# Linear attention: the gram, gram-query and row products, and the turned input behind them, made of rounded high and low parts

## The chip, the cores and the metric

The kernel runs on one core of one Trainium2 chip. Times are device microseconds of one execution. Beside the plain executions there is one execution recorded by the hardware profiler; rows and spans come from that one.

## The reference

The model is a chain of four layers on X with batch 2, 512 channels and 32x32 positions: deformable attention with an MLP, then a linear attention with a batch norm, then a non-local layer, then a rank-one layer. Only the second is touched:

```
K = conv1x1(X, Wq, bq); Q = conv1x1(X, Wk, bk); V = conv1x1(X, Wv, bv)   # 8 heads of 64 channels, n = 1024
M = einsum('bhmn,bhen->bhme', K, V)
Out = einsum('bhme,bhmn->bhen', M, Q)
Out = conv1x1(Out, Wo, bo) + X
Out = batch_norm over (batch, positions) * gamma + beta
```

There is no softmax between the products, so the kernel never makes K, Q and V. It makes the gram matrix G = X Xᵀ of each batch (512x512, over 1024 positions) and works with that.

## The kernel before

`stage_linear` does this layer. Its work is a list of tasks, `ORDER`, each one accumulation in one PSUM bank; task n uses bank n modulo 8. TensorE runs the list in order. VectorE and ScalarE run over the same list in the same order, and each empties the tasks that are its own. `emptied(engine, n)` makes an engine wait until task n has left its bank; TensorE calls it for task n−8, and for the tasks whose results it reads. Nothing else schedules: the order in the list is the order on every engine, and an engine that waits holds up all that stands behind it. The kinds of tasks, for each batch b:

- `turn` (8): four transposes of 128x128 turn 128 positions of X, so that positions lie on partitions; the copies go to `xt`.
- `gram` (4): row block i of G, columns i·128 to 512 only, so 512, 384, 256 and 128 columns wide, each a sum of 8 plain 32-bit products.
- `mirror` (3): transposes that fill the missing lower blocks of G.
- `row`: the sum of X over positions (`xs`, made by a reduction on VectorE) times Wq, one row.
- `times_q` (4): G times Wq, 4 plain products of 512 columns each; VectorE adds the bias term as it empties them into `gq`.
- `m`: Wv with `gq`, 16 plain products of 128 columns, and a rank-one term with the row `wrow`; VectorE copies the blocks of the heads into `mt`.
- `times_o`, `times_k`: with Wo, then with Wk. `bias_row`, `bias`: the bias that comes along. `y` (8): times X, plus X, with statistics for the batch norm.

Plain products take 32-bit operands. `times_k`, `bias_row` and `y` already work with parts: ScalarE writes a rounded copy of type fp32r (the high part), VectorE writes the operand less that copy, rounded too (the low part), and TensorE adds up high·high, low·high and high·low (`PAIRS`). A task whose result is needed in parts is emptied by both engines, first ScalarE (semaphore `high`), then VectorE.

The trace names memory, not the program's variables. `mlp_w`, `mlp_w_hi`, `Q` and `xn_a` are areas that the stage carves up: before, `xt` and `gram` lie in `mlp_w`, Wq, Wk, Wv and Wo in `mlp_w_hi`, the bias of Wq in `xn_a`. An `_r` behind a name is the same area in the rounded type. `lin_ps` are the eight banks.

Of the kernel before, what the change touches and what calls it, by code (L numbers as in the profile page):

```python
# [1287 lines left out]
def stage_linear(K, sb, ps):  # L1288
# [35 lines left out]
    mm, by_act, by_dve, summed = K.sem("lin_mm"), K.sem("lin_act"), K.sem("lin_dve"), K.sem("x_summed")  # L1324
    high, x_high, x_low, wk_split = K.sem("lin_high"), K.sem("x_high"), K.sem("x_low"), K.sem("wk_split")
# [14 lines left out]
    SPLIT = ("times_o", "times_k")  # L1340
    on_act = [k == "gram" or (k == "turn" and i % 2 == 1) for k, _, i in ORDER]

    def emptied(engine, n):

        engine.wait_ge(by_act if on_act[n] else by_dve, sum(on_act[m] == on_act[n] for m in range(n + 1)))


    TILE_AT = {("times_o", 0, 0): 0, ("times_q", 1, 2): 1, ("y", 0, 4): 2, ("y", 1, 0): 3}
# [5 lines left out]
    with nc.Block() as block:  # L1354
# [15 lines left out]
        def _(pe):  # L1370
            pe.wait_ge(w_in, 96)
            for n, (kind, b, i) in enumerate(ORDER):
# [11 lines left out]
                elif kind == "gram":  # L1384

                    need("turn", PC - 2, PC - 1)
                    for s in range(PC):
                        last = nc.tensor.matmul(out[:, i * P:], xt[b][:, s, i * P:(i + 1) * P], xt[b][:, s, i * P:],
                                                start=(s == 0), stop=(s == PC - 1))
                elif kind == "mirror":  # L1390
                    need("gram", i - 1)
                    for c in range(i):
                        last = nc.tensor.transpose(out[:, c * P:(c + 1) * P], gram[b][:, c, i * P:(i + 1) * P], K.k("ident"))
                elif kind == "row":
                    pe.wait_ge(summed, b + 1)
                    for c in range(CC):
                        last = nc.tensor.matmul(out[0:1, :], xs[:, b, c:c + 1], wq[:, c], start=(c == 0), stop=(c == CC - 1))
                elif kind == "times_q":
                    need("gram", CC - 1)
                    need("mirror", CC - 1)  # L1400
                    for c in range(CC):
                        last = nc.tensor.matmul(out[:], gram[b][:, c, i * P:(i + 1) * P], wq[:, c], start=(c == 0), stop=(c == CC - 1))
                elif kind == "m":
                    need("times_q", CC - 1)
                    need("row", 0)
                    for o in range(CC):
                        part = slice(o * P, (o + 1) * P)
# [25 lines left out]
                elif kind == "y":  # L1433
# [4 lines left out]
                    for c in range(CC):  # L1438
                        for k, (w, x) in enumerate(PAIRS):
                            last = nc.tensor.matmul(out[:], tt[w][:, c, o * P:(o + 1) * P], xp[tile % 2][x][:, c],  # L1440
# [4 lines left out]
        def _(dve):  # L1445
            dve.wait_ge(zero, 1)
            stats = 0
            for n, (kind, b, i) in enumerate(ORDER):
                src = bank[n % 8]
                if kind == "gram" and i == 0:  # L1450
                    nc.vector.tensor_reduce(xs[:, b], K.X[:, :, b], AX.X, ALU.add).then_inc(summed, 1)
                if (kind, b, i) in TILE_AT:
                    tile = TILE_AT[(kind, b, i)]
                    dve.wait_ge(x_high, tile + 1)
                    nc.vector.tensor_tensor(xp[tile % 2][1], x_tile(tile), xp[tile % 2][0].bitcast(F32), ALU.subtract).then_inc(x_low, 1)
# [720 lines left out]
```

## Time and profile before

| | us |
|---|---|
| median of 3 runs | 2783.54 (2780.62 to 2784.2) |
| profiled execution, its time | 2788.09 |
| profiled execution, its span | 2786.3 |
| TensorE busy | 2706.6 (97%) |
| VectorE busy | 2141.4 (77%) |
| ScalarE busy | 1671.4 (60%) |
| mean granted clock of TensorE | 0.99 |

The profiled execution took 2788.09 us, of which 1.8 us lie outside the span. In the rows below, PE is TensorE's products, PEld its loads of the stationary operand, DVE is VectorE, ACT is ScalarE, SP the engine that issues transfers. The first product of the stage starts at 2422.42 us and the first of the next stage at 2604.77 us. A matmul's record is longer than the time until the next one may start, since they run in a pipeline: what one costs in a sequence is the distance between starts.

### The profile page before, as it was taken

The page shows a single profiled execution, that of the slowest core. Times are in us where ns is not written, and L with a number is a line of the kernel's source. Part 1 is how long each engine was busy: PE and PEld are TensorE (multiplying, and loading weights), DVE is VectorE, ACT ScalarE, POOL GpSimd, SP SyncE. Part 2 cuts the span into 40 slices and gives each one's busy share as a digit, 9 for nine tenths or more (in the row PEclk, how much of TensorE's full clock was granted, in tenths as well). Part 3 has the DMA queues.
Part 4 walks back from the last instruction along what each step waited for, and adds up shares of the span by engine and source line. Part 5 has one row for each costly group of instructions (what it writes and reads, how often), then busy time and mean ns, then how long its engine had stood idle before and what let it go on. Part 6 is the DMA issues. An engine that isn't in the chain of part 4 may idle for free. (4 is left out here: it accounts for less than half of the span.)

```text
span 2786.3 us, 45961 instructions
## 1 busy us (share of the span) xinstructions
PE 2706.6 (97%) x20119; PEld 1352.0 (49%) x20119; DVE 2141.4 (77%) x1366; ACT 1671.4 (60%) x2601; POOL 95.4 (3%) x132
## 2 busy tenths in 40 slices
PE   6799999999999999999999999999899999999898
PEld 3434443443443334444444444444578888757653
DVE  4899999999999999999999999999642221224364
ACT  5777777777777777777777777776622222211244
POOL 3000000000000000000000000000431000000000
PEclk9899999999999999999999999999999999999999
DMA  2101000000000000000001010020500000200001
GB/s 72 57 16 30 9 30 30 16 30 9 30 30 16 30 9 30 30 16 30 9 30 30 16 30 9 30 43 1 170 1 1 1 0 1 86 0 1 1 1 61
DMA packets 38760, 72.26 MB, mean 26 GB/s; under 512 B 21088, under 2 KB 22048, under 8 KB 36896
## 3 DMA queue, kind: packets, MB, share of 16 engines
q1 hardware_dynamic: 38496, 69.19, 7.7%
q8 instruction: 158, 2.59, 0.4%
q14 instruction: 42, 0.34, 0.0%
q0 software_dynamic: 64, 0.13, 0.0%
HBM read 60.45 MB, written 8.86 MB: 25 GB/s over the span
## 5 line engine op out<-in xcount | busy, mean ns | idle before, releaser
L862 PE MATMUL l_ps<-mlp_w,W2H 128*64 128x512 f16 x5472 | 913.4, 392 | 1.7 <-DVE mlp_w L888 1.7
L927 ACT ACTIVATE relu_top<-l_ps 128x512 f32<-128x512 f32 x1024 | 611.9, 598 | 416.2 <-PE l_ps L862 371.0
L927 ACT ACTIVATE relu_bottom<-l_ps 128x512 f32<-128x512 f32 x1024 | 612.1, 598 | 79.6 <-PE l_ps L862 1.4
L770 DVE SCALAR_TENSOR_TENSOR relu_top<-relu_bottom,sign_ratio,relu_top 128x2048 f32<-128x2048 f32 x256 | 602.5, 2353 | 11.8 <-PEq L804 6.1
L862 PE MATMUL l_ps<-mlp_w,W2L 128*64 128x512 f16 x2736 | 536.2, 389 | 0.0
L862 PEld LDWEIGHTS l_ps<-mlp_w,W2H 128*64 128x64 f16 x5472 | 304.2, 108 | 357.5 <-issue 78.3
L862 PE MATMUL l_ps<-h_words,W2H 128*64 128x512 f16 x2720 | 453.1, 392 | 0.0
L888 DVE TENSOR_TENSOR mlp_w<-words_x,XN 128x2048 f32<-128x2048 f32 x172 | 392.2, 2292 | 24.6 <-PE l_ps L862 24.6
L888 DVE TENSOR_TENSOR mlp_w<-XN 128x2048 f32<-128x2048 f32 x170 | 387.7, 2294 | 19.3 <-PE l_ps L862 19.0
L862 PE MATMUL l_ps<-h_words,W2L 128*64 128x512 f16 x1360 | 266.1, 388 | 0.0
L764 PE MATMUL l_ps<-relu_top,W 128*32 128x512 f32 x2048 | 246.5, 598 | 0.0
L862 PEld LDWEIGHTS l_ps<-h_words,W2H 128*64 128x64 f16 x2720 | 151.0, 108 | 176.2 <-issue 38.3
L862 PEld LDWEIGHTS l_ps<-mlp_w,W2L 128*64 128x64 f16 x2736 | 153.1, 109 | 120.1 <-issue 0.8
L888 DVE TENSOR_TENSOR h_words<-XN 128x2048 f32<-128x2048 f32 x86 | 197.2, 2294 | 10.6 <-PE l_ps L862 10.6
L888 DVE TENSOR_TENSOR h_words<-words_x,XN 128x2048 f32<-128x2048 f32 x84 | 192.5, 2292 | 12.8 <-PE l_ps L862 12.8
L1280 DVE TENSOR_TENSOR KV_diag_r<-mlp_ps,KV_diag_r 128x512 fp32r<-128x512 f32 x43 | 29.7, 692 | 188.5 <-ACT mlp_ps L1262 188.5
L1261 ACT ACTIVATE KV_diag_r<-mlp_ps,vecs 128x512 fp32r<-128x512 f32 x43 | 29.6, 688 | 175.5 <-PE mlp_ps L1230 175.5
L764 PEld LDWEIGHTS l_ps<-relu_top,W 128*32 128x32 f32 x2048 | 53.2, 109 | 131.9 <-issue 129.0
L851 PE MATMUL l_ps<-XN,y_weights_halves 12*128 12x512 bf16 x1024 | 101.3, 385 | 7.8 <-PEq L382 7.8
L862 PEld LDWEIGHTS l_ps<-h_words,W2L 128*64 128x64 f16 x1360 | 76.0, 108 | 59.5
L851 PE MATMUL l_ps<-y_rows,y_weights_halves 12*128 12x512 bf16 x1024 | 101.1, 384 | 0.0
L851 PEld LDWEIGHTS l_ps<-XN,y_weights_halves 12*128 12x128 bf16 x1024 | 25.9, 91 | 143.6 <-issue 139.8
(392 smaller groups left out, 2695.9 us busy)
## 6 DMA issues: line engine op xcount, KB each, us to landing
XN<-pos_table SPq DMA_DIRECT2D x64, 512.0 KB, 3.8
mlp_w<-in_mlp_w SPq DMA_DIRECT2D x8, 1024.0 KB, 9.5
X<-in_x SPq DMA_DIRECT2D x8, 512.0 KB, 7.6
bias_scratch<-XN SPq DMA_DIRECT2D x64, 64.0 KB, 2.0
XN<-bias_scratch SPq DMA_DIRECT2D x16, 256.0 KB, 5.6
out<-Q SPq DMA_DIRECT2D x16, 256.0 KB, 2.2
XN<-y_pieces SPq DMA_DIRECT2D x96, 12.0 KB
y_rows<-y_pieces SPq DMA_DIRECT2D x96, 12.0 KB
```

Source lines behind the costliest of these rows:

```text
L764: last = nc.tensor.matmul(p3[32 * q:32 * q + 32, :], K.W3[:, 30 - 2 * n:62 - 2 * n], tops[i % 3][:, r, BANK * u:BANK * (u + 1)], start=(n ...
L770: nc.vector.scalar_tensor_tensor(tops[i % 3], bots[i % 2][:], K.RHO[:], tops[i % 3], ALU.mult, ALU.add).then_inc(folded, 1)
L851: last = nc.tensor.matmul(out[q][:], K.WYD[32 * q:32 * q + YROWS, q % 2], yr[bg % 2][32 * q:32 * q + YROWS, y] .unsqueeze(1).to_broadcast( ...
L862: last = nc.tensor.matmul(out[q][a * DH:(a + 1) * DH, :], w[:, half], h[a][:, :, k], start=False, stop=stop, tile_position=(0, a * DH))
L888: nc.vector.tensor_tensor(hw[i % 3][:, r].rearrange("p (m j) -> p m j", j=J), words_x, words_y[:, 2 * n + r].unsqueeze(1).to_broadcast([P, ...
L927: nc.scalar.activation((bots[i % 2] if d else tops[i % 3])[:, r, BANK * u:BANK * (u + 1)], banks[BANK_OF[c % PER]][:], ACT.Relu).then_inc( ...
L1261: nc.scalar.activation(hid[n % SLOTS][0], pa[n % 3][:], ACT.Gelu, bias=K.v("mlp_b1", f))
L1280: nc.vector.tensor_tensor(lo, pa[n % 3][:], hi.bitcast(F32), ALU.subtract).then_inc(lo_done, 1)
```

## The change

- `turn` and `gram` join the kinds that are emptied in two parts, by ScalarE and then VectorE. Before, ScalarE emptied all `gram` tasks and every second `turn` task alone, VectorE the other `turn` tasks. The high parts of the turned X lie in `Q`, the low ones in `mlp_w`.
- `gram` and `times_q` are three products of parts for each plain one. Wq is split for it, once: the high part by ScalarE before gram (1,0), the low part by VectorE before the first mirror of batch 0.
- `mirror` turns both parts: 6 tasks a batch instead of 3.
- `row` is one task for both batches. `xs` now holds the sums of batch 0 in column 0 and of batch 1 in column 32 of 33, the rest zeros, so that the two results land on partitions 0 and 32. It too is three products of parts. It stands directly in front of `m` of batch 0.
- The two reductions over X move from before gram (0,0) and (1,0) to before gram (0,2) and (1,1) in VectorE's order.
- The last six `turn` tasks of batch 1 move between the grams of batch 0.
- The split of tile 1 of X for `y` moves from `times_q` (1,2) to `times_k` (0,0), since its memory holds a part of the gram until then.
- All waits on emptied tasks now count VectorE's semaphore alone.

```
+    low, rest = carver(K.w_lo), carver(K.w_hi2)
+    xt = [[low([P, PC, C]) for _ in range(B)], [rest([P, PC, C]) for _ in range(B)]]
+    gram = [[low([P, CC, C]) for _ in range(B)], [aT[1], xp[0][0]]]
+    wqp = [carver(K.w_hi2)([P, CC, C]), K.w_hi[:, 0:2].rearrange("p f a o -> p (f a) o")]
...
-    ORDER = (tasks("turn", 0, *range(PC)) + tasks("turn", 1, *range(PC)) + tasks("gram", 0, *range(CC)) + tasks("row", 0, 0)
-             + tasks("gram", 1, 0) + tasks("mirror", 0, *range(1, CC)) + tasks("gram", 1, 1) + tasks("times_q", 0, *range(CC))
-             + tasks("gram", 1, 2, 3) + tasks("m", 0, 0) + tasks("row", 1, 0) + tasks("mirror", 1, *range(1, CC))
+    MIRROR = [(k, part) for k in range(1, CC) for part in range(2)]
+    ORDER = (tasks("turn", 0, *range(PC)) + tasks("turn", 1, *range(2)) + tasks("gram", 0, 0) + tasks("turn", 1, *range(2, 5))
+             + tasks("gram", 0, 1) + tasks("turn", 1, *range(5, PC)) + tasks("gram", 0, 2, 3)
+             + tasks("gram", 1, 0) + tasks("mirror", 0, *range(len(MIRROR))) + tasks("gram", 1, 1) + tasks("times_q", 0, *range(CC))
+             + tasks("gram", 1, 2, 3) + tasks("row", 0, 0) + tasks("m", 0, 0) + tasks("mirror", 1, *range(len(MIRROR)))
...
-    SPLIT = ("times_o", "times_k")
+    SPLIT = ("turn", "gram", "times_o", "times_k")
...
-                    need("turn", PC - 2, PC - 1)
+                    need("turn", PC - 1)
                     for s in range(PC):
-                        last = nc.tensor.matmul(out[:, i * P:], xt[b][:, s, i * P:(i + 1) * P], xt[b][:, s, i * P:],
-                                                start=(s == 0), stop=(s == PC - 1))
+                        for k, (w, x) in enumerate(PAIRS):
+                            last = nc.tensor.matmul(out[:, i * P:], xt[w][b][:, s, i * P:(i + 1) * P], xt[x][b][:, s, i * P:],
+                                                    start=(s == 0 and k == 0), stop=(s == PC - 1 and k == 2))
...
-                    pe.wait_ge(summed, b + 1)
+                    pe.wait_ge(summed, B + 3)
+                    pe.wait_ge(wq_split, 2)
                     for c in range(CC):
-                        last = nc.tensor.matmul(out[0:1, :], xs[:, b, c:c + 1], wq[:, c], start=(c == 0), stop=(c == CC - 1))
+                        for k, (w, x) in enumerate(PAIRS):
+                            last = nc.tensor.matmul(out[0:33, :], xsp[w][:, c], wqp[x][:, c], start=(c == 0 and k == 0), stop=(c == CC - 1 and k == 2))
...
-                        last = nc.tensor.matmul(out[:], gram[b][:, c, i * P:(i + 1) * P], wq[:, c], start=(c == 0), stop=(c == CC - 1))
+                        for k, (w, x) in enumerate(PAIRS):
+                            last = nc.tensor.matmul(out[:], gram[w][b][:, c, i * P:(i + 1) * P], wqp[x][:, c],
+                                                    start=(c == 0 and k == 0), stop=(c == CC - 1 and k == 2))
...
-                    need("row", 0)
+                    emptied(pe, AT[("row", 0, 0)])
...
+                if (kind, b, i) in (("gram", 0, 2), ("gram", 1, 1)):
+                    nc.vector.tensor_reduce(xs[:, :, b, 0], K.X[:, :, b], AX.X, ALU.add).then_inc(summed, 1)
...
+                if (kind, b, i) == ("mirror", 0, 0):
+                    dve.wait_ge(wq_split, 1)
+                    nc.vector.tensor_tensor(wqp[1], wq, wqp[0].bitcast(F32), ALU.subtract).then_inc(wq_split, 1)
```

The beginning of the stage on TensorE, before (L1383 is `turn`, L1388 `gram`, L1397 `row`, L1393 `mirror`):

```order
L1383 MATMUL lin_ps<-consts_sb,X 128x128 x64
L1388 MATMUL lin_ps<-mlp_w 128x512 x8
L1388 MATMUL lin_ps<-mlp_w 128x384 x8
L1388 MATMUL lin_ps<-mlp_w 128x256 x8
L1388 MATMUL lin_ps<-mlp_w 128x128 x8
L1397 MATMUL lin_ps<-mlp_w_hi,x_sums 1x512 x4
L1388 MATMUL lin_ps<-mlp_w 128x512 x8
```

The same place after (L1399 is `turn`, L1405 `gram`; a gram task of 8 steps is eight times the three rows):

```order
L1399 MATMUL lin_ps<-consts_sb,X 128x128 x40
L1405 MATMUL lin_ps<-mlp_w_r 128x512
L1405 MATMUL lin_ps<-mlp_w_r,Q_r 128x512
L1405 MATMUL lin_ps<-Q_r,mlp_w_r 128x512
...
L1399 MATMUL lin_ps<-consts_sb,X 128x128 x12
L1405 MATMUL lin_ps<-mlp_w_r 128x384
```

Gram (0,0) now follows ten turn tiles instead of sixteen, and every plain product is three.

VectorE in the front part of the stage, before (L1464 empties `turn`, L1451 sums X, L1458 and L1459 make low parts of the bias and of Wk, L1468 empties `row`, L1466 `mirror`, L1471 `times_q`):

```order
L1464 COPY mlp_w<-lin_ps 128x512 x8
L1451 TENSOR_REDUCE x_sums<-X 128x4
L1458 TENSOR_TENSOR bk_part<-vecs,bk_part 128x4
L1459 TENSOR_TENSOR mlp_w_hi_r<-mlp_w_hi,xn_a_r 128x2048
L1468 SCALAR_TENSOR_TENSOR wq_s<-xn_a,lin_ps 1x512
L1451 TENSOR_REDUCE x_sums<-X 128x4
L1466 COPY mlp_w<-lin_ps 128x128
L1466 COPY mlp_w<-lin_ps 128x256
L1466 COPY mlp_w<-lin_ps 128x384
L1471 SCALAR_TENSOR_TENSOR mlp_w<-xn_a,x_sums,lin_ps 128x512 x4
```

And after, from gram (0,2) on (L1477 sums X, L1509 writes low parts, L1483 the low part of Wq, L1495 empties `mirror`, L1500 `times_q`):

```order
L1477 TENSOR_REDUCE x_sums<-X 128x4
L1509 TENSOR_TENSOR mlp_w_r<-lin_ps,mlp_w_r 128x256
L1509 TENSOR_TENSOR mlp_w_r<-lin_ps,mlp_w_r 128x128
L1509 TENSOR_TENSOR mlp_w_r<-lin_ps,mlp_w_r 128x512
L1483 TENSOR_TENSOR mlp_w_hi_r<-mlp_w_hi,Q_r 128x2048
L1495 CAST mlp_w_r<-lin_ps 128x128 x2
L1495 CAST mlp_w_r<-lin_ps 128x256 x2
L1495 CAST mlp_w_r<-lin_ps 128x384 x2
L1477 TENSOR_REDUCE x_sums<-X 128x4
L1509 TENSOR_TENSOR mlp_w_r<-lin_ps,mlp_w_r 128x384
L1500 SCALAR_TENSOR_TENSOR mlp_w<-xn_a,x_sums,lin_ps 128x512 x4
```

The low part of Wq and six mirror copies now stand between gram (1,0) and the second sum over X.

TensorE around `m` of batch 0, before (L1409 and L1410 are `m`, L1402 `times_q`; four pairs of the two `m` rows):

```order
L1388 MATMUL lin_ps<-mlp_w 128x128 x8
L1409 MATMUL lin_ps<-mlp_w,mlp_w_hi 128x128 x4
L1410 MATMUL lin_ps<-wq_s,xn_a 128x128
...
L1397 MATMUL lin_ps<-mlp_w_hi,x_sums 1x512 x4
L1393 MATMUL lin_ps<-consts_sb,mlp_w 128x128 x6
L1402 MATMUL lin_ps<-mlp_w_hi,mlp_w 128x512 x8
```

And after (L1417 is `row`, L1433 and L1434 `m`, L1411 `mirror`, L1424 `times_q`):

```order
L1417 MATMUL lin_ps<-Q_r,x_sums_part 33x512 x2
L1417 MATMUL lin_ps<-mlp_w_hi_r,x_sums_part 33x512
...
L1433 MATMUL lin_ps<-mlp_w,mlp_w_hi 128x128 x4
L1434 MATMUL lin_ps<-wq_s,xn_a 128x128
...
L1411 MATMUL lin_ps<-consts_sb,mlp_w_r 128x128 x12
L1424 MATMUL lin_ps<-Q_r,mlp_w_r 128x512 x2
```

The row task stood behind `m` of batch 0 for batch 1; now it stands in front of it, and `m` is followed at once by the transposes.

## Rows read from the trace of the kernel before

**Rows 1.** The page: busy time, then busy tenths and granted clock in 40 slices.

```profile
PE 2706.6 (97%) x20119; PEld 1352.0 (49%) x20119; DVE 2141.4 (77%) x1366; ACT 1671.4 (60%) x2601; POOL 95.4 (3%) x132
...
PE   6799999999999999999999999999899999999898
...
PEclk9899999999999999999999999999999999999999
```

**Rows 2.** Timeline, TensorE: start us, length us, engine, line, operation, shapes, count, idle before.

```profile
2422.42 10.15 PE L1383 MATMUL lin_ps<-consts_sb,X 128*128 128x128 f32 x64 [3.09 <-PEq L1200]
...
2432.41 17.43 PE L1388 MATMUL lin_ps<-mlp_w 128*128 128x512 f32 x64
2449.77 3.59 PE L1397 MATMUL lin_ps<-mlp_w_hi,x_sums 128*1 128x512 f32 x8
2453.29 7.13 PE L1388 MATMUL lin_ps<-mlp_w 128*128 128x512 f32 x16
2460.26 0.82 PE L1393 MATMUL lin_ps<-consts_sb,mlp_w 128*128 128x128 f32 x6
2460.92 5.32 PE L1388 MATMUL lin_ps<-mlp_w 128*128 128x384 f32 x16
2466.08 13.90 PE L1402 MATMUL lin_ps<-mlp_w_hi,mlp_w 128*128 128x512 f32 x32
2479.82 5.40 PE L1388 MATMUL lin_ps<-mlp_w 128*128 128x256 f32 x32
...
2490.96 3.59 PE L1397 MATMUL lin_ps<-mlp_w_hi,x_sums 128*1 128x512 f32 x8
...
2496.41 7.11 PE L1402 MATMUL lin_ps<-mlp_w_hi,mlp_w 128*128 128x512 f32 x16 [1.05 <-DVE mlp_w L1466]
```

**Rows 3.** Timeline, TensorE, products of rounded parts: `times_k` (L1419) and `y` (L1440).

```profile
2513.89 0.39 PE L1419 MATMUL lin_ps<-aT_hi,mlp_w_hi_r 128*128 128x512 f32 x1
...
2524.61 0.39 PE L1419 MATMUL lin_ps<-mlp_w_r,xn_a_r 128*128 128x512 f32 x1
...
2575.35 22.04 PE L1440 MATMUL lin_ps<-mlp_w_r 128*128 128x512 f32 x96 [0.55 <-DVE lin_bias L1484]
```

**Rows 4.** Weight loads: timeline; then groups (count, busy us, mean ns, idle before).

```profile
2479.82 5.21 PEld L1388 LDWEIGHTS lin_ps<-mlp_w 128*128 128x128 f32 x31 [0.24 <-issue]
...
L1419 PEld LDWEIGHTS lin_ps<-aT_hi,xn_a_r 128*128 128x128 f32 x32 | 6.0, 188 | 1.6 <-issue 0.2
```

**Rows 5.** Timeline, VectorE: sum of X, low part of Wk, evictions.

```profile
2432.78 4.41 DVE L1451 TENSOR_REDUCE x_sums<-X 128x4 f32<-128x4096 f32 x1
...
2437.18 2.28 DVE L1459 TENSOR_TENSOR mlp_w_hi_r<-mlp_w_hi,xn_a_r 128x2048 fp32r<-128x2048 f32 x1
...
2453.40 0.68 DVE L1468 SCALAR_TENSOR_TENSOR wq_s<-xn_a,lin_ps 1x512 f32<-1x512 f32 x1 [13.94 <-PE lin_ps L1397]
...
2491.07 0.42 DVE L1475 COPY mt<-lin_ps 64x256 f32<-64x256 f32 x1 [10.30 <-PE lin_ps L1410]
...
2495.20 1.07 DVE L1466 COPY mlp_w<-lin_ps 128x128 f32<-128x128 f32 x3
...
2506.42 2.48 DVE L1480 TENSOR_TENSOR mlp_w_r<-lin_ps,aT_hi 128x512 fp32r<-128x512 f32 x4
```

**Rows 6.** Timeline, ScalarE: turn tiles 4, 6, 8 and 10 leave their banks.

```profile
2426.11 0.60 ACT L1528 ACTIVATE mlp_w<-lin_ps 128x512 f32<-128x512 f32 x1 [1.11 <-PE lin_ps L1383]
2427.81 0.60 ACT L1528 ACTIVATE mlp_w<-lin_ps 128x512 f32<-128x512 f32 x1 [1.11 <-PE lin_ps L1383]
2429.10 0.60 ACT L1528 ACTIVATE mlp_w<-lin_ps 128x512 f32<-128x512 f32 x1 [0.69 <-PE lin_ps L1383]
2429.98 0.60 ACT L1528 ACTIVATE mlp_w<-lin_ps 128x512 f32<-128x512 f32 x1 [0.28 <-PE lin_ps L1383]
```

**Rows 7.** Busy us (count) of stretches; then granted clock, DMA share, GB/s.

```profile
2422.37:2432.35 9.98, 9.93 (x64) 9.96 (x65) 5.02 (x8) 4.18 (x7) 0.52 (x1) 0.69 0.42 127
2432.35:2449.77 17.42, 17.42 (x68) 10.94 (x65) 7.11 (x4) 3.97 (x6) 0.00 (x0) 1.00 0.00 0
```

More of the change, by code:

```diff
@@ L1303, in stage_linear @@
     room = carver(K.WR)
-    xt, gram = [room([P, PC, C]) for _ in range(B)], [room([P, CC, C]) for _ in range(B)]
+    room([P, B * (PC + CC), C])
     gq = room([P, CC, C])
-    room([P, CC, C])
     mt = sb("mt", [P, CC, P])
@@ L1339, in stage_linear, with parts @@
     PAIRS = ((0, 0), (1, 0), (0, 1))
-    SPLIT = ("times_o", "times_k")
-    on_act = [k == "gram" or (k == "turn" and i % 2 == 1) for k, _, i in ORDER]
+    SPLIT = ("turn", "gram", "times_o", "times_k")
     def emptied(engine, n):
-        engine.wait_ge(by_act if on_act[n] else by_dve, sum(on_act[m] == on_act[n] for m in range(n + 1)))
-    TILE_AT = {("times_o", 0, 0): 0, ("times_q", 1, 2): 1, ("y", 0, 4): 2, ("y", 1, 0): 3}
+        engine.wait_ge(by_dve, n + 1)
+    def parts(kind, b, i):
+        if kind == "turn":
+            return [xt[p][b][:, i] for p in range(2)]
+        if kind == "gram":
+            return [gram[p][b][:, i, i * P:] for p in range(2)]
+        return [{"times_o": aT, "times_k": tt}[kind][p][:, i] for p in range(2)]
+    TILE_AT = {("times_o", 0, 0): 0, ("times_k", 0, 0): 1, ("y", 0, 4): 2, ("y", 1, 0): 3}
+    FREE = {0: ("gram", 1, CC - 1), 1: ("times_q", 1, CC - 1), 2: ("y", 0, CC - 1), 3: ("y", 0, 2 * CC - 1)}
+    xsum = flat(xs[:]).rearrange("p (c k) -> p c k", c=CC)[:, :, 0:33]
     def x_tile(tile):
@@ L1390, in _ @@
                 elif kind == "mirror":
-                    need("gram", i - 1)
-                    for c in range(i):
-                        last = nc.tensor.transpose(out[:, c * P:(c + 1) * P], gram[b][:, c, i * P:(i + 1) * P], K.k("ident"))
+                    k, part = MIRROR[i]
+                    need("gram", k - 1)
+                    for c in range(k):
+                        last = nc.tensor.transpose(out[:, c * P:(c + 1) * P], gram[part][b][:, c, k * P:(k + 1) * P].bitcast(F32), K.k("ident"))
@@ L1409, in _ @@
                             nc.tensor.matmul(out[:, part], wv[:, c, part], gq[:, c, part], start=(c == 0), stop=False)
-                        last = nc.tensor.matmul(out[:, part], bvr[0:1, part], wrow[:, part], start=False, stop=True)
+                        last = nc.tensor.matmul(out[:, part], bvr[at, part], wrow[at, part], start=False, stop=True)
                 elif kind == "times_o":
@@ L1439, in _ @@
                         for k, (w, x) in enumerate(PAIRS):
[L1440 removed]
+                            last = nc.tensor.matmul(out[:], tt[w][:, c, o * P:(o + 1) * P], xp[(tile + 1) % 2][x][:, c],
                                                     start=(c == 0 and k == 0), stop=(c == CC - 1 and k == 2))
@@ L1446, in _ @@
             dve.wait_ge(zero, 1)
+            nc.vector.memset(xs[:], 0.0).then_inc(summed, 1)
+            dve.wait_ge(summed, 1)
             stats = 0
@@ L1477, in _ @@
                 elif kind in SPLIT:
-                    part = {"times_o": aT, "times_k": tt}[kind]
+                    part = parts(kind, b, i)
                     dve.wait_ge(high, sum(k in SPLIT for k, _, _ in ORDER[:n + 1]))
-                    nc.vector.tensor_tensor(part[1][:, i], src[:], part[0][:, i].bitcast(F32), ALU.subtract).then_inc(by_dve, 1)
+                    nc.vector.tensor_tensor(part[1], src[:, i * P if kind == "gram" else 0:], part[0].bitcast(F32), ALU.subtract).then_inc(by_dve, 1)
                 elif kind == "bias_row":
@@ L1522, in _ @@
                 src = bank[n % 8][:]
-                if on_act[n]:
+                if kind in SPLIT:
                     act.wait_ge(mm, n + 1)
-                    if kind == "gram":
-                        nc.scalar.activation(gram[b][:, i, i * P:], src[:, i * P:], ACT.Copy).then_inc(by_act, 1)
-                    else:
-                        nc.scalar.activation(xt[b][:, i], src, ACT.Copy).then_inc(by_act, 1)
-                elif kind in SPLIT:
-                    act.wait_ge(mm, n + 1)
-                    nc.scalar.activation({"times_o": aT, "times_k": tt}[kind][0][:, i], src, ACT.Copy).then_inc(high, 1)
+                    nc.scalar.activation(parts(kind, b, i)[0], src[:, i * P if kind == "gram" else 0:], ACT.Copy).then_inc(high, 1)
             N_ST = CC * B * NT + CC
```

44 lines of the change are left out of this document (26 added, 18 removed).

## The prediction, made before the changed kernel ran

> **What bounds the kernel now.** The page came first. TensorE is busy for 97% of the span, and its granted clock is nine tenths or more in 39 of 40 slices [rows 1]. So time leaves the kernel where TensorE's own work gets shorter, and comes in where it waits. The diff touches one stage, the linear attention, which runs from 2422.4 us to about 2604.8 us. Next I read the timeline of TensorE in that stage [rows 2]. The reader is to see that its records follow each other without a hole from 2422.42 to 2496.41, where the only wait in the part that changes stands: 1.05 us, for VectorE's mirror copies. VectorE and ScalarE are mostly idle there: in 17.42 us of the first gram products VectorE works 7.11 us and ScalarE 3.97 us [rows 7]. So extra evictions have room, unless someone waits for them.
>
> **The price of a product.** A plain 32-bit product leaves two records in the trace. The 16 records of 384 columns from 2460.92 to 2466.08 are 0.3225 us apart, and 16 of 256 plus 16 of 128 columns take 5.23 us from 2479.82 to 2485.05: plain records scale with the columns, 0.429, 0.322, 0.215 and 0.107 us for 512, 384, 256 and 128 (0.429 from the 32 in the 13.74 us from 2466.08); the six transposes at 2460.26, (0.82−0.27)/5, are 0.11 us apiece [rows 2]. A product of rounded parts leaves one record. In the products that are split already (48 of `times_k`, 46 steps from 2513.89 to 2524.61) it takes 10.72/46 = 0.233 us; in `y` (95 steps in 22.04 minus one length of 0.39) 0.228 us [rows 3]. Three of them for 512 columns cost 0.70 us against 0.858 us plain: 18% less, not a third.
>
> All those rows have 512 columns. At 2.4 GHz, 512 columns are 0.213 us, so 0.020 us is left over for each. I take the same surplus for narrower ones: 0.180 us for 384 and 0.127 us for 256 columns. For 128 columns that would be 0.073 us, but each product has a weight load of its own, and 31 loads of 128 columns went by in 5.21 us at steps down to 0.107 us beside the plain records [rows 4]; no row shows them closer. I take 0.107 us. The bounds: from below, 0.053 us (pure streaming at 128 columns); from above, what a whole plain product of that width costs, 0.215 us for 128 and 0.429 us for 256 columns.
>
> The Trainium skill ("TensorE: Matmul & The Clock Gate", "LDWEIGHTS (loading the stationary operand)") puts a load at its columns over 1.2 GHz, 107 ns for 128; the trace's loads last 188 ns each but follow at 0.107 us, which agrees with it as a rate. The same page ("Back-to-back issue gap") gives columns over 2.4 GHz plus 2.5 ns, 216 ns for 512; the rows have 228 to 233 ns. The measurement decides.
>
> **Part by part, on TensorE.**
> - `times_q`: 32 products of 512 columns. 64 records of 0.429 us are 27.5 us; 96 of 0.233 us are 22.4 us. −5.1 us.
> - `row`: two tasks of 3.52 us each (2449.77 to 2453.29, and again at 2490.96) [rows 2] become one of 12 records, 2.8 us. −4.2 us.
> - `gram`: 16 products of each width. 512: 13.7 to 11.2 us. 384: 10.3 to 8.6. 256: 6.9 to 6.1. 128: 3.4 to 5.1, dearer, since three loads take the place of two records. Together −3.3 us.
> - `mirror`: both parts are transposed, 12 transposes more at 0.11 us. +1.3 us.
> - `turn`: the same 64 transposes. `m`, `times_o`, `times_k`, `y`: untouched.
>
> **The waits that it adds.** Every turn and gram tile now passes through ScalarE (high part, 0.60 us) and then VectorE (low part, 0.69 us; back to back (2.48−0.69)/3 = 0.60 us each [rows 5]), where before one of them copied it. In the opening (granted clock 0.69 over the first 10 us [rows 7]) two turn tiles take TensorE 1.70 us, 2426.11 to 2427.81 [rows 6], 0.85 us each, so the two keep up.
> - Gram of batch 0 now starts after ten turn tiles and needs tile 8. ScalarE began on that tile at 2429.10 and on the tenth at 2429.98 [rows 6]. So the high part ends at 2429.70, the low part at 2430.5, TensorE resumes at 2430.6, and has been idle since 2429.8: +0.8 us. The six turn tiles put between the grams cost what they cost before.
> - `m` of batch 0 stands directly behind `row`, and waits for VectorE's 0.68 us on it [rows 5]. The record's end lags TensorE's next start by 0.16 us; with about 0.15 us of hand-over that is +1.0 us. Before, gram products and others lay between. Queued behind that wait is all of TensorE.
> - Before `times_q` of batch 1 six mirror copies stand where three stood: three take 1.07 us. From the end of `m`: 0.1, the two copies of `mt` 0.85, six copies 2.1, hand-over 0.1, 3.2 us; TensorE's transposes end at 1.5. A wait of 1.7 us instead of 1.05: +0.7 us.
> - Batch 0's `times_q` has cover, just: from the end of gram (1,0), its low part is done at +1.3 us, the low part of Wq (2.28 us as for Wk [rows 5]) at +3.6, six copies at +5.7; TensorE has mirrors 1.3 and gram (1,1) 4.3, so 5.6 us. About 0. What comes late here goes onto the path one for one.
> - The two sums over X (4.41 us each [rows 5]) now stand before the low parts of gram (0,2) and gram (1,1). The first hides behind the rest of that gram and the 5.6 us of gram (1,0), the second behind four `times_q` of 2.8 us and free banks. 0, and up to 4.4 us each without that cover.
> - The memset, the parts of the sums (128x132) and Wq's high part lie beside TensorE's work: 0.
> - The split of x tile 2 moves from `times_q` to `times_k` of batch 0; its first user is `y` of the second tile, over 20 us later: 0. No DMA moves.
>
> Sum: −5.1 −4.2 −3.3 +1.3 +0.8 +1.0 +0.7 = **−8.8 us**. The stage behind 2513.25 slides forward unchanged. Against the profiled execution, 2788.1 us with its frame, that gives 2779.3 us; the median of the runs shown is 4.5 us lower, so 2774.7 us.
>
> **The rivals.**
> 1. *Narrow rounded products cost a whole plain product at 128 columns.* Nothing in the trace shows a rounded product below 512 columns. At 0.215 us instead of 0.107 for 48 records: +5.2 us, gain 3.6 us, 2779.9 us. For: they are weight-bound there already and nothing shows the rate. Against: the loads of plain records do better.
> 2. *The penalty reaches 256 columns too.* 48 records at 0.429 instead of 0.127 us: another +14.5 us; in all +10.9 us, 2794.4 us, slower. It decides once the 96 records of 256 and 128 columns cost 0.092 us more each than I take.
> 3. *VectorE becomes the bound in the front part.* It gets about 16 turn low parts, 8 gram low parts, 6 more mirror copies and Wq, some 20 us more in 70 us. If the tight place before `times_q` slips by 3 us, the gain is 5.8 us: 2777.7 us.
> 4. *Loads do not bind.* 128 columns at 0.053 us (−2.6 us) and 0.228 us or its surplus elsewhere (252 records by 0.005, −1.3 us): gain 12.7 us, 2770.8 us. The skill's issue-gap rule, cited above, points this way: by it the sum would be some 4 us better than mine even with loads at 107 ns. Rows 3 speak against it.
> 5. *The change does not do what it says.* The order of instructions shows 192 gram products and 96 of `times_q`, each with rounded operands on both sides, so only the rate can fail.
>
> **How the numbers follow.** Forecast (−8.8 us) 45%, rival 1 32%, rival 2 7%, rival 3 10%, rival 4 6%. The three runs before spread over 3.6 us, so I widen the ends by 1 to 2 us: 2771 to 2782.5 us holds the forecast, rivals 1 and 3 and half of 4. About 0.2% (5.6 us) is what a measurement of this kernel tells from no change. Faster by more: nearly all of the forecast, half of 3, all of 4: 52%. Within: nearly all of 1, half of 3, a little of the forecast: 38%. Slower: rival 2 and a rest: 10%.
>
> **What would show it.** In the changed trace: `times_k` starts at about 2504.5 instead of 2513.25 us. Gram records 0.233, 0.18, 0.127 and 0.107 us apart by width; 0.21 at 128 is rival 1, 0.4 at 256 rival 2. Waits of TensorE of about 0.8 us before the first gram record, 1.0 before `m`, 1.7 before `times_q` of batch 1, and none over 0.3 before that of batch 0. A low granted clock behind 2430 us would make all of it wrong, as would a lasting queue of full banks.

## The result, and the profile after

| | before | after |
|---|---|---|
| median of 14 runs each | 2783.36 us (2780.62 to 2785.43) | 2775.42 us (2773.24 to 2778.83) |
| profiled execution | 2788.09 us | 2777.56 us |
| its span | 2786.3 us | 2775.7 us |
| first transpose of the stage to second `times_k` record | 2422.42 to 2513.89 = 91.47 us | 2422.08 to 2503.21 = 81.13 us |

The changed kernel takes 0.9972 of the time before, 95% interval 0.9964 to 0.9979: 7.9 us less, 5.8 to 10.0. The forecast was 8.8 us less, 2774.7 us.

The page of after, first part (busy us, share, instructions):

```profile
PE 2693.2 (97%) x20223; PEld 1364.2 (49%) x20223; DVE 2153.3 (78%) x1390; ACT 1678.5 (60%) x2611; POOL 95.4 (3%) x132
```

Against [rows 1], TensorE has 104 records more and 13.4 us less busy time. VectorE has 24 instructions and 11.9 us more. A count of instructions alone says nothing here: a wide rounded record costs less than one of the two that a plain product leaves (0.227 for 0.429 us at 512 columns, below).

TensorE's timeline in the stage, after (columns as in [rows 2]):

```profile
2422.08 5.91 PE L1399 MATMUL lin_ps<-consts_sb,X 128*128 128x128 f32 x40 [3.08 <-PEq L1200]
2429.44 0.47 PE L1405 MATMUL lin_ps<-mlp_w_r 128*128 128x512 f32 x1 [1.45 <-DVE Q_r L1509]
...
2432.51 0.39 PE L1405 MATMUL lin_ps<-mlp_w_r,Q_r 128*128 128x512 f32 x1
...
2434.78 0.39 PE L1405 MATMUL lin_ps<-Q_r,mlp_w_r 128*128 128x512 f32 x1
2435.01 1.48 PE L1399 MATMUL lin_ps<-consts_sb,X 128*128 128x128 f32 x12
...
2437.91 0.33 PE L1405 MATMUL lin_ps<-mlp_w_r 128*128 128x384 f32 x1
...
2440.17 0.33 PE L1405 MATMUL lin_ps<-mlp_w_r,Q_r 128*128 128x384 f32 x1
...
2442.07 0.28 PE L1405 MATMUL lin_ps<-Q_r,mlp_w_r 128*128 128x256 f32 x1
...
2444.58 0.28 PE L1405 MATMUL lin_ps<-Q_r,mlp_w_r 128*128 128x256 f32 x1
...
2444.88 0.27 PE L1405 MATMUL lin_ps<-Q_r,mlp_w_r 128*128 128x128 f32 x1
...
2447.22 0.28 PE L1405 MATMUL lin_ps<-Q_r,mlp_w_r 128*128 128x128 f32 x1
...
2458.91 0.70 PE L1424 MATMUL lin_ps<-Q_r,mlp_w_r 128*128 128x512 f32 x2 [0.37 <-DVE mlp_w_r L1495]
...
2475.42 0.62 PE L1417 MATMUL lin_ps<-Q_r,x_sums_part 128*33 128x512 f32 x2
...
2477.95 0.40 PE L1417 MATMUL lin_ps<-mlp_w_hi_r,x_sums_part 128*33 128x512 f32 x1
2479.21 1.13 PE L1433 MATMUL lin_ps<-mlp_w,mlp_w_hi 128*128 128x128 f32 x8 [0.86 <-DVE wq_s L1497]
...
2485.19 1.54 PE L1411 MATMUL lin_ps<-consts_sb,mlp_w_r 128*128 128x128 f32 x12
...
2488.52 0.70 PE L1424 MATMUL lin_ps<-Q_r,mlp_w_r 128*128 128x512 f32 x2 [1.80 <-DVE mlp_w_r L1495]
...
2494.07 3.60 PE L1437 MATMUL lin_ps<-mlp_w_hi,mt 128*128 128x512 f32 x8
...
2503.21 0.39 PE L1443 MATMUL lin_ps<-aT_hi,mlp_w_hi_r 128*128 128x512 f32 x1
```

Start minus start, divided by the steps between two records of one width, is the price of a product of rounded parts:

| columns | rows | steps | us each | forecast | two plain records, a third of it |
|---|---|---|---|---|---|
| 512 | 2432.51 to 2434.78 | 10 | 0.227 | 0.233 | 0.286 |
| 384 | 2437.91 to 2440.17 | 13 | 0.174 | 0.180 | 0.215 |
| 256 | 2442.07 to 2444.58 | 21 | 0.120 | 0.127 | 0.143 |
| 128 | 2444.88 to 2447.22 | 21 | 0.111 | 0.107 | 0.074 |

The last column is the price at which the split would break even. The three wide forms are under it, the narrowest one is above it: there the split loses. The steps are those of the even part of each task. Over the whole of a task, from its first record to the first one behind it, the 24 products of each width took 5.57, 4.27, 2.95 and 2.63 us, so 0.232, 0.178, 0.123 and 0.110 us each: the first wide products of a task stand further apart.

The group of waits says where TensorE stands idle in the stage (us in total, times, longest); before, it had only one wait in the part that changes [rows 2]:

```profile
PE lin_ps L1399 <- PEq L1200: 3.1, 1, 3.1
PE lin_ps L1424 <- DVE mlp_w_r L1495: 2.2, 2, 1.8
PE lin_ps L1405 <- DVE Q_r L1509: 1.4, 1, 1.4
PE lin_ps L1433 <- DVE wq_s L1497: 0.9, 1, 0.9
```

The first is there before the change too and stands ahead of the stage's first transpose. The other three lines are four waits, together 4.5 us, against 1.05 us before. All four are for VectorE.

### The profile page after: what moved, and what is told of

It reads as the page before. It is cut to its first block and busy times, and to the rows that moved or that the text cites. A ratio compares the mean times of both kernels' runs of the same rounds, so it can differ in the third digit from the quotient of the medians.

```text
span 2775.7 us, 46239 instructions
## 1 busy us (share of the span) xinstructions
PE 2693.2 (97%) x20223; PEld 1364.2 (49%) x20223; DVE 2153.3 (78%) x1390; ACT 1678.5 (60%) x2611; POOL 95.4 (3%) x132
## 5 line engine op out<-in xcount | busy, mean ns | idle before, releaser
L770 DVE SCALAR_TENSOR_TENSOR relu_top<-relu_bottom,sign_ratio,relu_top 128x2048 f32<-128x2048 f32 x256 | 601.2, 2348 | 11.9 <-PEq L804 6.1
```

What stands on the lines that cost most here:

```text
L770: nc.vector.scalar_tensor_tensor(tops[i % 3], bots[i % 2][:], K.RHO[:], tops[i % 3], ALU.mult, ALU.add).then_inc(folded, 1)
```

## The experiments

Each ran beside the kernel before on the same chip. The edits named "on after" start from the changed kernel, "on before" from the kernel before. Two measures are used. The ratio of medians has an interval of 2 to 4 us on either side. The stage front, from the first transpose to the second record of `times_k` in one profile, is finer and holds all that the change touches. It holds the moment at which the granted clock rises as well: in eleven of the twelve profiles 2.8 to 3.7 us after the stage's first transpose, in the first profile of before 6.1 us after it.

### Both kernels again

No edit.

> The kernel before, unchanged, profiled once more. The changed kernel's turn tiles reached the full granted clock about 3.5 us earlier than in the first profile of before (40 transposes in 5.9 us, where before needed about 7.4 us for them). Theory: that moment varies from run to run, and the change has nothing to do with it; then this profile may show another moment than 2428.4 us. Rival: the change brings it forward; then this profile again shows the half clock until about 2428 us, and 64 transposes in 9.9 to 10.2 us.

> The changed kernel, unchanged. Time 7.0 to 8.5 us under before. If the moment of the clock's rise varies by itself, the 40 first transposes may take anything from 5.9 to 7.4 us here, and the wait before the first gram product then goes the other way, 1.45 us with an early rise and 0.8 us with a late one; the stage up to times_k then takes 80.9 to 81.7 us. If the change brings it forward, they take 5.9 us again.

Measured: 2782.28 us (one run), and 2775.96 us, ratio 0.997 [0.996, 0.9981]. Stage front 89.96 and 81.10 us. Before, again, TensorE's timeline:

```profile
2419.88 8.65 PE L1383 MATMUL lin_ps<-consts_sb,X 128*128 128x128 f32 x64 [3.08 <-PEq L1200]
...
2509.84 0.39 PE L1419 MATMUL lin_ps<-aT_hi,mlp_w_hi_r 128*128 128x512 f32 x1
```

The same 64 transposes took 10.15 us in the first profile [rows 2]. The granted clock explains it. Windows of before again, then of the first profile of before (window; its length; busy us and count of PE, PEld, DVE, ACT, POOL; granted clock; DMA share; GB/s):

```profile
2421.80:2422.80 1.00, 1.00 (x7) 1.00 (x6) 0.09 (x1) 0.60 (x1) 0.00 (x0) 0.50 0.85 320
2422.80:2423.80 1.00, 1.00 (x11) 1.00 (x10) 0.65 (x2) 0.49 (x1) 0.00 (x0) 0.96 0.90 256
```

```profile
2426.00:2428.00 2.00, 2.00 (x12) 2.00 (x11) 0.69 (x1) 0.78 (x2) 0.00 (x0) 0.50 0.87 284
2428.00:2430.00 2.00, 2.00 (x17) 2.00 (x17) 1.15 (x2) 1.03 (x3) 0.00 (x0) 0.88 0.06 19
```

In the first profile the clock was at 0.50 (1.2 GHz) until about 2428.5 (0.48 us of the stretch from 2428 give its mean of 0.88), 6.1 us after the first transpose. In before again it rose 3.0 us after it, in after 2.8 us. So 1.5 us of the 10.3 us between the first two profiles (91.47 − 81.13) is a late rise in one execution. With the early rise in both, the change takes 89.96 − 81.10 = **8.9 us** out of the stage front.

### Plain products put back, gram alone and `times_q` alone

On after:

```diff
-for k, (w, x) in enumerate(PAIRS):
-    last = nc.tensor.matmul(out[:, i * P:], xt[w][b][:, s, i * P:(i + 1) * P], xt[x][b][:, s, i * P:], ...)
+last = nc.tensor.matmul(out[:, i * P:], xt[0][b][:, s, i * P:(i + 1) * P].bitcast(F32), xt[0][b][:, s, i * P:].bitcast(F32), ...)
```

> The changed kernel, but each gram product is one plain 32-bit product on the high part of X alone; the low parts of X are made and not used, so the gram lacks them. Theory: TensorE's rate is what counts. Plain records cost 0.858, 0.644, 0.429 and 0.215 us a product, three rounded ones in the changed kernel's trace 0.683, 0.520, 0.360 and 0.334 us; 16 products of each: +2.8, +2.0, +1.1 and -1.9 us, together +4.0 us over the changed kernel; 0.4 us of it are taken back, since the wait before times_q of batch 0 vanishes. So 4.2 us under before. Rival, that the gain of the gram was eaten by waits and evictions: no slower than the changed kernel, 7.9 us under before.

And for the other:

```diff
-for k, (w, x) in enumerate(PAIRS):
-    last = nc.tensor.matmul(out[:], gram[w][b][:, c, i * P:(i + 1) * P], wqp[x][:, c], ...)
+last = nc.tensor.matmul(out[:], gram[0][b][:, c, i * P:(i + 1) * P].bitcast(F32), wqp[0][:, c].bitcast(F32), ...)
```

> The changed kernel, but times_q is one plain product for each, on the high parts of the gram and of Wq; the low parts are made and not used there. Theory: 32 products at 0.858 instead of 0.683 us, +5.6 us over the changed kernel, 2.3 us under before. Rival, that times_q waits for VectorE's evictions or the sums over X and not for its own products: under +2 us.

Measured: gram plain 2779.19 us (0.9983 [0.9974, 0.9993]), 3.2 us above after again; stage front 86.28 us, 5.2 us more. `times_q` plain 2780.99 us (0.9988 [0.9979, 0.9998]), 5.0 us above; stage front 86.78 us, 5.7 us more. The 16 products of batch 0 are one row of TensorE's timeline, 32 records in 13.97 us, as in the kernel before (13.90 [rows 2]), and the wait ahead is the one of after:

```profile
2456.63 13.97 PE L1423 MATMUL lin_ps<-Q_r,mlp_w_r 128*128 128x512 f32 x32 [0.37 <-DVE mlp_w_r L1493]
```

The profile of gram plain did not fit its own median (2782.16 for 2779.19 us). The surplus is not in the gram. It stands in the windows behind the wait before `times_q` of batch 1 (columns as in the windows above):

```profile
2492.00:2494.00 2.00, 1.44 (x6) 1.25 (x7) 0.30 (x1) 0.00 (x0) 0.00 (x0) 0.97 0.00 0
2494.00:2496.00 2.00, 2.00 (x6) 1.52 (x6) 0.00 (x0) 0.00 (x0) 0.00 (x0) 0.50 0.00 0
2496.00:2498.00 2.00, 2.00 (x8) 1.57 (x7) 0.75 (x1) 0.00 (x0) 0.00 (x0) 0.67 0.00 0
2498.00:2500.00 2.00, 2.00 (x10) 1.60 (x9) 0.05 (x1) 0.00 (x0) 0.00 (x0) 1.00 0.00 0
```

TensorE's timeline at that place, of the same kernel:

```profile
2492.56 0.71 PE L1423 MATMUL lin_ps<-Q_r,mlp_w_r 128*128 128x512 f32 x2 [1.80 <-DVE mlp_w_r L1494]
...
2494.98 0.63 PE L1423 MATMUL lin_ps<-mlp_w_hi_r,mlp_w_r 128*128 128x512 f32 x1
```

The granted clock fell to 0.50 for about 3.4 us, and the records got longer (0.63 for 0.39 us). That cost 1.65 us: the two `times_q` tasks took 7.19 us (2492.56 to 2499.75) instead of the 5.55 us of after. Is it caused by plain gram products, or does it come and go? The same kernel was run again for that:

> The variant with plain gram products on the high parts, profiled once more. In its first profile the granted clock fell to half for 3.4 us behind TensorE's wait of 1.8 us, which cost 1.65 us; four profiles with the same wait had no such fall. Theory: chance decides, and this profile most likely shows none, with 84.6 us from the first transpose to the second record of times_k instead of 86.3 us. Rival: this kernel always has it, then 86.3 us again.

Measured: 2781.05 us (one run), stage front 84.67 us, 3.57 us above after again, and no fall of the clock.

```profile
2421.58 6.23 PE L1399 MATMUL lin_ps<-consts_sb,X 128*128 128x128 f32 x40 [3.08 <-PEq L1200]
...
2506.25 0.39 PE L1442 MATMUL lin_ps<-aT_hi,mlp_w_hi_r 128*128 128x512 f32 x1
```

So the split of `times_q` is worth 5.7 us and that of the gram 3.6 us. The 3.6 us are net: with plain gram products the wait ahead of `times_q` of batch 0 is gone, and with split ones it costs 0.5 us. The same edit ran without the fall of the clock, so the edit does not force it.

### The row product once, on before

```diff
-+ tasks("gram", 0, *range(CC)) + tasks("row", 0, 0)
++ tasks("gram", 0, *range(CC))
...
-+ tasks("gram", 1, 2, 3) + tasks("m", 0, 0) + tasks("row", 1, 0) + tasks("mirror", 1, ...)
++ tasks("gram", 1, 2, 3) + tasks("row", 0, 0) + tasks("m", 0, 0) + tasks("mirror", 1, ...)
...
-last = nc.tensor.matmul(out[0:1, :], xs[:, b, c:c + 1], wq[:, c], ...)
+last = nc.tensor.matmul(out[0:33, :], xsum[:, c], wq[:, c], ...)
```

> The kernel before with one part of the change alone: the row product made once for both batches (33 columns, plain products), in front of m of batch 0. Theory, with the steps of the prediction: the second row task goes (-3.5 us), m now waits for VectorE's eviction of the row (+1.0 us), and the wait before times_q of batch 1 grows by 0.2 us, since no row covers the mirror copies: -2.3 us, 2781.2 us if before is 2783.5. Rival, merging is free of new waits: -3.5 us. Rival, it pays nothing, because the second row had hidden the mirror copies: 0.

Measured: 2783.59 us, 0.9997 [0.9988, 1.0007], which is −0.3 us with an interval of −3.3 to +1.9. By the median this part alone can't be told from nothing. Its stage front is 87.89 us against 89.96 of before again, −2.1 us. The granted clock rose 3.7 us after the first transpose here, for 3.0 us, and the 64 transposes took 0.2 us longer (8.70 for 8.49 us, start to start): −2.3 us at an equal opening, as forecast. TensorE's timeline:

```profile
2478.18 3.62 PE L1399 MATMUL lin_ps<-mlp_w_hi,x_sums 128*33 128x512 f32 x8
...
2482.67 1.13 PE L1412 MATMUL lin_ps<-mlp_w,mlp_w_hi 128*128 128x128 f32 x8 [0.86 <-DVE wq_s L1473]
...
2490.88 7.11 PE L1404 MATMUL lin_ps<-mlp_w_hi,mlp_w 128*128 128x512 f32 x16 [1.35 <-DVE mlp_w L1471]
```

One row product of 33 stationary columns takes 3.62 us, as long as one of a single column (3.59 [rows 2]). The second one goes. Behind the one that is left there is the wait for VectorE, 0.86 us, and the wait before `times_q` of batch 1 is longer (1.35 for 1.05 us). −3.5 us for the product that goes, and about 1.2 us back in two waits.

### The waits taken away by order

Row product ahead of the last gram task, and the mirrors ahead of `m`, on after:

```diff
-+ tasks("gram", 1, 2, 3) + tasks("row", 0, 0) + tasks("m", 0, 0) + tasks("mirror", 1, *range(len(MIRROR)))
++ tasks("gram", 1, 2) + tasks("row", 0, 0) + tasks("gram", 1, 3) + tasks("mirror", 1, *range(len(MIRROR))) + tasks("m", 0, 0)
```

> The changed kernel with another order: gram (1,2), row, gram (1,3), the six mirrors of batch 1, and only then m of batch 0. Theory: the waits of 0.86 us (m for the row) and 1.80 us (times_q of batch 1 for the mirror copies) are pure loss and both go: 2.7 us under the changed kernel, 2773.3 us, 10.2 us under before. In the trace no wait of TensorE over 0.2 us between gram (1,2) and times_o. Rival: the waits come back elsewhere (at gram (1,3)'s bank, or at times_q of batch 1 for the low part of gram (1,3)): gain under 1 us.

Five turn tiles of batch 1 ahead of the first gram, and Wq's low part made later on VectorE, on after:

```diff
-+ tasks("turn", 1, *range(2)) + tasks("gram", 0, 0) + tasks("turn", 1, *range(2, 5)) + tasks("gram", 0, 1)
++ tasks("turn", 1, *range(5)) + tasks("gram", 0, 0) + tasks("gram", 0, 1)
...
-if (kind, b, i) == ("mirror", 0, 0):
+if (kind, b, i) == ("gram", 1, 0):
     dve.wait_ge(wq_split, 1)
```

> The changed kernel with five turn tiles of batch 1 instead of two before gram (0,0), and VectorE's low part of Wq before its low part of gram (1,0). Theory: TensorE does three more turn tiles (1.3 us) while it waits for VectorE's low part of tile 8, so of the wait of 1.4 us 0.1 to 0.2 us are left; and the 0.37 us before times_q of batch 0 go: 1.6 us under the changed kernel, 2774.4 us. Rival: VectorE is the bound of the opening, and gram (0,1) then waits for what it has to do: gain under 0.5 us.

Both together:

> The changed kernel with both reorderings. If they are independent, 4.3 us under the changed kernel: 2771.7 us, 11.8 us or 0.42% under before. If the two sets of waits share a cause, no better than the better of the two. In a profile of another variant the granted clock fell to half for 3.4 us right behind the wait of 1.8 us, at a cost of 1.6 us; without that wait no such fall can stand there, so the mean gain may be larger than the sum of the waits.

| | median | ratio to before | stage front | against after again (81.10) | expected |
|---|---|---|---|---|---|
| row and mirrors moved | 2772.84 | 0.9959 [0.9946, 0.9973] | 78.12 | −3.0 | −2.7 |
| turn tiles and Wq moved | 2774.50 | 0.9968 [0.9956, 0.9980] | 79.28 | −1.8 | −1.6 |
| all moved | 2769.98 | 0.9949 [0.9937, 0.9962] | 76.12 | −5.0 | −4.3 |

What the two give adds up (3.0 + 1.8 = 4.8 of 5.0 us): the waits are separate and none was hidden behind another. With all moved, the group of TensorE's waits in the stage has one line left, the one ahead of it:

```profile
PE lin_ps L1399 <- PEq L1200: 3.1, 1, 3.1
```

TensorE's timeline of all moved shows the four places without a bracket, so without idle time over 0.15 us ahead: the first gram record, `times_q` of batch 0, `m` behind the mirrors, and `times_q` of batch 1:

```profile
2420.16 7.30 PE L1399 MATMUL lin_ps<-consts_sb,X 128*128 128x128 f32 x52 [3.08 <-PEq L1200]
2427.52 0.47 PE L1405 MATMUL lin_ps<-mlp_w_r 128*128 128x512 f32 x1
...
2455.14 0.63 PE L1424 MATMUL lin_ps<-Q_r,mlp_w_r 128*128 128x512 f32 x2
...
2474.31 1.50 PE L1411 MATMUL lin_ps<-consts_sb,mlp_w_r 128*128 128x128 f32 x12
...
2475.65 1.06 PE L1433 MATMUL lin_ps<-mlp_w,mlp_w_hi 128*128 128x128 f32 x8
...
2481.55 0.73 PE L1424 MATMUL lin_ps<-Q_r,mlp_w_r 128*128 128x512 f32 x2
```

This is the version that beats both kernels: 2769.98 us (2768.98 to 2770.98), some 14 us below the 2783.93 of before beside it, and 5.4 us below the 2775.42 of after (which had before at 2783.36 beside it). VectorE does the same work in it, only not while TensorE stands waiting.

### What the narrowest product waits for

Is the 0.111 us of a 128-column product its weight load? On after, the narrowest gram task loads half as many columns; all 128 columns still stream. The lower half of that gram block is left out, so the time is that of less data loaded, not of the reference's work. The edit halves the output rows along with the load; the two are not told apart.

```diff
+m = P // 2 if i == CC - 1 else P
...
-last = nc.tensor.matmul(out[:, i * P:], xt[w][b][:, s, i * P:(i + 1) * P], xt[x][b][:, s, i * P:], ...)
+last = nc.tensor.matmul(out[0:m, i * P:], xt[w][b][:, s, i * P:i * P + m], xt[x][b][:, s, i * P:], ...)
```

> The changed kernel, but the products of the narrowest gram tasks (128 columns) load only 64 of the 128 stationary columns; the lower half of that block of the gram is left out. In the changed kernel's trace these records are 0.111 us apart, 256 columns 0.120, 384 columns 0.173 and 512 columns 0.2275: all but the narrowest are columns over 2.4 GHz plus 0.0135 us, which would give 0.067 us for 128. Theory: the narrowest wait for their weight loads; with half the load they come down to about 0.067 us. Rival, a floor per product that has nothing to do with the load: 0.111 us as before.

Measured: 2771.68 us (one run), stage front 78.71 us, 2.4 us less than after again. TensorE's timeline, the narrowest gram task:

```profile
2441.86 0.22 PE L1406 MATMUL lin_ps<-mlp_w_r 128*64 128x128 f32 x1
...
2443.24 0.23 PE L1406 MATMUL lin_ps<-Q_r,mlp_w_r 128*64 128x128 f32 x1
```

23 steps in 1.38 us, 0.060 us each, where the same moving columns took 0.111 us. So the stationary width, and not the moving one, sets the pace at 128 columns. What sets it at 0.060 us is open: half the load and 128 streamed columns come to the same 0.053 us. And 0.060 is less than the 0.067 us that the expectation made of the surplus of 0.0135 us, so that surplus does not hold for every form. The loads of that line (shortest, median and longest ns of one record):

```profile
L1406 PEld LDWEIGHTS lin_ps<-mlp_w_r x64: 134/188/192, 2426.6 to 2469.9; 128*128 128x128 f32 x48, 128*64 128x64 f32 x16
```

A load's record of 188 ns is much longer than the 111 ns between loads, so its length is no price: the next one begins before it ends. The Trainium skill ("TensorE: Matmul & The Clock Gate", "LDWEIGHTS (loading the stationary operand)") puts a load at its columns over 1.2 GHz, so 107 and 53 ns. Steps of 111 and 60 ns are 4 and 13% above that.

## Why the prediction was right, point by point

| term | forecast | measured | from |
|---|---|---|---|
| `times_q` | −5.1 | −5.3 to −5.7 | two tasks in 5.55 us (2488.52 to 2494.07), four such pairs, against 27.5; and `times_q` plain |
| row once and split | −4.2 | −4.3 | 2.76 us for 7.04; 12 records from 2475.42 |
| gram | −3.3 | −3.9, −3.6 | its four tasks 15.42 for 17.36 us in a batch; gram plain, net of the wait behind it |
| mirrors | +1.3 | +1.3 | batch 1: 12 transposes in 1.54 us (row at 2485.19) for 6 in 0.87; batch 0: 1.48 for 0.82 |
| wait before gram (0,0) | +0.8 | +1.4 to +1.6 | row at 2429.44; 1.6 by starts |
| wait before `times_q`, batch 0 | 0 | +0.5 | last gram record at 2458.21 plus a step of 0.17, to 2458.91 |
| `m` behind row | +1.0 | +1.0 | 2477.95 plus one step, 2478.18, to the start of `m` at 2479.21 |
| wait before `times_q`, batch 1 | +0.7 | +0.75 | 1.80 for 1.05 us |
| sum | −8.8 | −8.4 to −9.0 | stage front at equal clock: −8.9 |

An idle time in brackets counts from the end of a record, about 0.16 us behind the moment at which the next one could have started, so a wait that is new costs that much more than its bracket: 0.53 us for 0.37, 1.03 for 0.86.

That the sum agrees to 0.1 us is luck in part. The products came out cheaper than forecast by 0.6 us in the gram and 0.2 to 0.6 us in `times_q`, and two waits dearer by 0.6 to 0.8 and 0.5 us; the errors took each other out.

**The price of wide rounded products.** The method was right: take the surplus over pure streaming from a row that exists, and carry it to widths that no row shows. The surplus was mis-sized. It is 0.0135 us rather than 0.020 in the even part of a task: 0.227, 0.174 and 0.120 us are 512, 384 and 256 columns at 2.4 GHz (0.213, 0.160, 0.107) plus 0.0135. The row that I took it from (0.233 [rows 3]) and `y` in the same group (0.228) already disagreed. I took the dearer one, and the cheaper one was the general case. Here it was worth 0.6 us of the gram term.

**The narrow product.** Bound by the stationary side, 0.111 us for a forecast of 0.107. The forecast read the plain records too low: those of 128 columns do not stand 0.107 us apart, and 0.215 us is not the price of a product. In the kernel before, the last gram task of batch 1 has 15 steps from 2483.27 to 2484.94, 0.1115 us each and 0.223 us a product, and its loads follow each other at 0.110 to 0.112 us. So the trace of before held the measured rate. The 0.107 came out of the assumption that plain records scale with their columns down to 128. Rival 1 (0.215) is excluded by the rows, and rival 2 (0.429 at 256 columns) as well. The half load shows that the cause is on the stationary side. Rival 4 fell with its main term: narrow products do not run at 0.053 us. Its smaller one, a surplus of less than 0.020 us, was right.

**The first wait.** The step that failed is "the two keep up", and the time 2430.5 for the low part behind it. It was worked out from [rows 6], taken in an execution whose clock rose late: there two turn tiles take TensorE 1.70 us, slower than VectorE's 0.60 us for each. In after the clock rose 2.8 us after the first transpose, TensorE ran through its 40 opening transposes in 5.91 us, and VectorE's low parts became the limit. Its timeline, after:

```profile
2425.61 4.88 DVE L1509 TENSOR_TENSOR Q_r<-lin_ps,mlp_w_r 128x512 fp32r<-128x512 f32 x8 [0.17 <-ACT mlp_w_r L1560]
```

Eight of them, for tiles 3 to 10, stand back to back, 4.88/8 = 0.61 us each, while TensorE at full clock makes a tile of four transposes in 0.44 us (row at 2435.01: (1.48−0.27)/11 = 0.11 us apiece). The sixth is tile 8's, which gram (0,0) needs: it ends at 2429.30, and TensorE resumes at 2429.44. In gram plain again the clock rose later, 3.7 us after the first transpose, and the 40 transposes took 6.23 us; the first gram record came 7.4 us after the first transpose as in after, and only the wait was shorter, 1.18 us. A row that was read at half clock had been used for a stretch at full clock. It was 0.6 to 0.8 us. This wait and the next are the places where rival 3 (VectorE as the bound) was partly true.

**Batch 0's `times_q`.** "Just" covered, 5.6 against 5.7 us, and warned of as one for one. VectorE's timeline, after:

```profile
2453.78 0.69 DVE L1509 TENSOR_TENSOR mlp_w_r<-lin_ps,mlp_w_r 128x512 fp32r<-128x512 f32 x1 [5.18 <-PE lin_ps L1411]
2454.38 2.28 DVE L1483 TENSOR_TENSOR mlp_w_hi_r<-mlp_w_hi,Q_r 128x2048 fp32r<-128x2048 f32 x1
2456.58 2.08 DVE L1495 CAST mlp_w_r<-lin_ps 128x128 fp32r<-128x128 f32 x6
2458.57 4.42 DVE L1477 TENSOR_REDUCE x_sums<-X 128x4 f32<-128x4096 f32 x1
...
2485.72 0.43 DVE L1505 COPY mt<-lin_ps 64x256 f32<-64x256 f32 x1
2486.18 2.08 DVE L1495 CAST mlp_w_r<-lin_ps 128x128 fp32r<-128x128 f32 x6
```

The links of the chain are as long as forecast: Wq's low part 2.28 us, six copies 2.08 us. The gram's end is the start of TensorE's mirrors, 2452.87. The low part of gram (1,0) was done 1.6 us behind it (2454.47) for a forecast of 1.3, but each instruction starts before the record of the last one ends, and the copies were done at 2458.66, 5.8 us behind it for a forecast of 5.7. The cover was 5.5 for 5.6 us, with gram (1,1) at the cheaper price. And TensorE begins at 2458.91, behind a hand-over of 0.25 us that the sum had not reckoned for here. From 5.5 to 6.04 us, that is 0.54 us by starts, 0.37 us in the bracket. The sum over X that follows (4.42 us) is not waited for, as forecast. In batch 1 the six copies end at 2488.26, TensorE begins at 2488.52, and the wait is 1.80 us for a forecast of 1.7.

**The frame.** The sum was subtracted from an execution with a late clock rise, 2788.1 us, and the result put back by 4.5 us to the median. Its stage front was 1.5 us longer for that reason alone; by the stage front of before again (89.96) nothing is owed to it. The shift by 4.5 us to the median took that out.

Medians give 7.9 us (5.8 to 10.0) and the stage front 8.9. The difference is within the interval, but the profiles also show where time comes back. From the second `times_k` record to the next stage's first product after and after again take 0.2 us less than the two of before. From there to the end they take more:

| | before | before again | after | after again |
|---|---|---|---|---|
| next stage's first product to the end, us | 181.5 | 179.8 | 181.8 | 181.9 |
| granted clock, 2560 to 2630 us | 0.95 | 0.95 | 0.93 | 0.93 |
| granted clock, 2690 to 2730 us | 0.91 | 0.96 | 0.91 | 0.91 |

In code that the change does not touch, after spends longer at a granted clock of 0.50, and the second pair gives back 2.1 of the 8.9 us there, the first pair 0.3 us. Whether the change brings that about or the executions differ by chance stays open: `times_q` plain, made from after, took 179.8 us there, and the other variants of after 180.6 to 182.2 us.

## What to carry to other kernels

Three products of rounded parts beat a plain 32-bit product only where the moving side is wide: here 20% less at 512 columns (0.68 for 0.858 us), 19% at 384 and 16% at 256, but 50% more at 128 (0.334 for 0.223 us), where the stationary side sets the pace. The split's by-products, two evictions a tile and twice the transposes, are hidden only if something else stands between them and their reader; an order that puts other tiles there was worth 5.0 us beside the 8.9 us of the change. Read a producer's pace at the clock that its stretch will have, and sort chains by how tightly they are covered: the two that I called covered "just" and "keeping up" are the two that came late.

## What the hardware did that I had not expected

The granted clock rises at different moments in executions of the same program. In the first profile of before it stayed at 0.50 until 6.1 us after the stage's first transpose, in before again until 3.0 us, while TensorE did the same transposes; in the other ten profiles it rose after 2.8 to 3.7 us. That alone moves the stage by 1.5 us, a sixth of the change's effect.

It can fall too: in gram plain it went to 0.50 for 3.4 us, about 1.3 us after TensorE had resumed behind the 1.80 us wait, and cost 1.65 us. In six other profiles with the same wait (after, after again, gram plain again, `times_q` plain, turn tiles moved, half load) it stayed up. A wait of that length may thus cost nearly double its own time in some executions. That the wait brought the fall about is argued from its place alone, from one case in seven; with all moved there is no such wait.

The row product with 33 stationary columns took 3.62 us and with one column 3.59 us: for plain 32-bit operands with 512 moving columns the stationary width was free.
